# Attention and slot mixture on one core: one PSUM bank per product, ScalarE rounds the pair sums, and four engines get new orders

## The chip, the core and the metric

One core of a Trainium2 chip runs the whole program. Its engines work side by side, each through its own list of instructions in order: TensorE (PE, with weight loads as PEld), VectorE (DVE), ScalarE (ACT), GpSimd (POOL) and SyncE (SP, which here only issues transfers). They meet at semaphores. PSUM has eight banks of 2 KB per partition, in which PE leaves its products and which ACT and DVE read. The metric is the device time of one execution in microseconds; lower is better.

## The reference

```python
x = L0_attn_x                                        # 32 x 256 x 128
# attention, linear and causal: 16 heads of 8
q, k, v = exp(ln(x) @ Wq.T + bq), exp(ln(x) @ Wk.T + bk), ln(x) @ Wv.T + bv
kv = cumsum(k[..., :, None] * v[..., None, :], over the sequence); k1 = cumsum(k)
att = (q @ kv) / (q . k1)
x = x + ln(att @ Wo.T + bo)
# slot mixture: 8 experts x 64 slots = 512 slots
xn, se = rms_norm(ln(x)), rms_norm(slot_embeds)
logits = xn @ se.T                                   # 256 x 512
slots = softmax(logits, over tokens).T @ xn
processed = gelu(slots @ w1) @ w2
x = x + ln(softmax(logits, over slots) @ processed)
```

All is float32. There are 32 batches of 256 tokens.

## The kernel before

A batch is one unit of work. Its 256 tokens lie on 128 partitions, two neighbours (an even and an odd token) on each. A product that has to be exact is split: an operand is rounded to a high part (`_hi`) and the rest is its low part (`_lo`), and `three` multiplies hi by hi, hi by lo and lo by hi. Each engine's program is a list of calls such as `hidden(n, f)`, where `n` is the batch. `first_steps` and `last_steps` write out the ends of the program, and `step(s)` the steady part. One step works on up to seven batches at different stages.

One batch passes through the engines so. DVE takes the statistics of x (`x_statistics`), POOL makes 1/sqrt of the variance (`x_rstd_of`, an operation on two numbers per partition), DVE normalises (`x_normalise`), PE transposes (`x_transpose`), ACT copies the rounded part (`xT_high`) and DVE the rest (`xT_low`). `project` makes q, k and v, `v_evict` and `qk_evict` (with exp) move them to `E`. SP then copies the odd tokens' keys and values one partition further down, into `prev` (`shift_odd`, two transfers of 112 and 15 KB). POOL makes the outer products of keys and values (`outer_even`, `outer_odd`), adds them (`pair_sum`, `pair_keys`) into `kv` (128 x 1152), copies it rounded to `kv_hi` (`sums_high`) and subtracts (`sums_low`). `cumulate` multiplies both with a triangle, in three parts k = 0, 1, 2. DVE multiplies each part by q (`multiply`) and sums over the head (`attention_sums`), and `attention` divides. `att_transpose`, `attT_copy` and `attention_out` follow, then the squares on ACT (`y_squares`), the power on POOL (`y_rstd_of`), `first_residual` on DVE, and the same for the second normalisation: `x1_squares`, `x1_rstd_of`, `x1_normalise`, `xn_transpose`, `xnT_high`, `xnT_low`.

The mixture goes on with `logits`, the two maxima on DVE (`slot_maxima`, `part_maxima`), `dispatch_exp` on ACT, `dispatch_scale` on DVE, `dispatch_transpose`, `dispatch_copy` on ACT, `gather_slots`, `slT_high` (ACT), `slT_low` (DVE), `hidden` in four parts with a `gelu` each, `process`, `proc_copy`, `mixture` and, after one more set of squares and power, `second_residual`. ACT loads a table before the first gelu of a step and again before the exps (`gelu_table`, `exp_table`).

PSUM is held as four pairs of banks: WB, LA, LB and HB. WB serves `x_transpose`, `att_transpose`, `project`, `part_transpose`, `attention_out`, `cumulate`, `xn_transpose` and the sums of the attention, one after another. So `project(n, 1)` waits until ACT has copied the transposed attention of batch n - 2 out of the bank:

```python
elif c == 1:
    after(pe, attT_ready, n - 2)
...
three(WB[:, c, 0:QKV], xT_hi[:, cols], xT_lo[:, cols], wqkv_hi[:, :], wqkv_lo[:, :])
```

`hidden` uses the two banks of HB in turn, so parts 2 and 3 wait for the gelus of parts 0 and 1. `wait_ge(s, v)` is a wait, `then_inc` an engine's signal on completion, and `after(eng, s, n)` waits until batch n has signalled `s`. In an order, `waits s_attT` means `attT_ready`, and so on.

Of the kernel before, what the change touches and what calls it, by code (L numbers as in the profile page):

```python
# [5 lines left out]
def attention_and_slot_mixture(  # L6
# [45 lines left out]
    with ctx:  # L52
# [6 lines left out]
        def sem(name):  # L59
# [89 lines left out]
        LBv = LB[:, :, :].rearrange("p g (j t) -> p (g j) t", t=SEQ)  # L149
        OB = LA[:, :, 0:YW]  # L150
        PR = HB[:, 0, :].rearrange("p (j d) -> p j d", d=DIM)
        ND = WB[:, 1, 0:NC * (HD + 1) * NH].rearrange("p (c f h) -> p c f h", c=NC, h=NH)
        YB = WB[:, 1, 0:NC * YW].rearrange("p (c d) -> p c d", d=YW)
# [3 lines left out]
        s_wT, s_woT, s_wop, s_wu, s_sesum, s_senorm, s_kappa = (  # L157
            sem("s_" + n) for n in ("wT", "woT", "wop", "wu", "sesum", "senorm", "kappa"))
        s_gxs, s_sefloor, s_sehi, s_wqkvhi, s_wqkv, s_w1hi, s_wo_t = (
            sem("s_" + n) for n in ("gxs", "sefloor", "sehi", "wqkvhi", "wqkv", "w1hi", "wo_t"))  # L160
# [15 lines left out]
        xT_lo_ready, qk_exp, kv_even, kv_odd, kv_den, kv_built = (  # L176
            sem("s_" + n) for n in ("xTlo", "qkexp", "kve", "kvo", "kvd", "kv"))
        kv_hi_ready, kv_lo_ready, qk_own_ready, own_den, own_ready, own_added = (
            sem("s_" + n) for n in ("kvhi", "kvlo", "qkown", "ownden", "own", "ownadd"))
        summed, den_ready, att_ready, att_T, attT_ready, wo_done = (  # L180
            sem("s_" + n) for n in ("summed", "deninv", "att", "attTp", "attT", "wo"))
        y_var, y_rstd, x1_ready, x1_var, x1_floor, x1_rstd = (
            sem("s_" + n) for n in ("yve", "yrs", "x1", "x1ve", "x1fl", "x1rs"))
        xn_ready, xnT_done, xnT_hi_ready, xnT_lo_ready, lb_done, part_ready = (
            sem("s_" + n) for n in ("xn", "xnT", "xnThi", "xnTlo", "lb", "part"))
        partT_done, tok_ready, lb_shifted, disp_exp, disp_inverted, disp_scaled = (
            sem("s_" + n) for n in ("partT", "tok", "lbs", "dexp", "dinv", "dscale"))
        slT_done, slT_hi_ready, slT_lo_ready, proc_ready, mix_done, o_var = (
            sem("s_" + n) for n in ("slT", "slThi", "slTlo", "procs", "mix", "ove"))
        o_rstd, res_ready, x_stat = (  # L190
            sem("s_" + n) for n in ("ors", "res", "xstat"))
# [28 lines left out]
        def _(sp):  # L220
# [43 lines left out]
        def _(pool):  # L264
# [17 lines left out]
            def x_rstd_of(n):  # L282
                pool.wait_ge(x_stats, n + 1)
                if n == 2:
                    after(pool, xh_ready, n - 1)
# [9 lines left out]
            def wo_order():  # L295
                pool.wait_ge(s_woload, 16)
                pool.tensor_copy(wo_p[:, :].rearrange("p (d h) -> p d h", d=HD),
                                 w_in[:, 3, :].rearrange("p (h d) -> p d h", d=HD)).then_inc(s_wop, 1)

            def slot_norms():  # L300
                pool.wait_ge(s_sesum, 1)
# [5 lines left out]
            @each_batch  # L307
            def sums_high(n):
                after(pool, cum_done[2], n - 1)
                if n == 1:  # L310
                    pool.wait_ge(kv_den, n + 1)
                pool.wait_ge(kv_built, n + 1)
                pool.tensor_copy(kv_hi[:, :], kv[:, :]).then_inc(kv_hi_ready, 1)
# [8 lines left out]
            def own_value(n):  # L322
                pool.wait_ge(own_den, n + 1)
# [30 lines left out]
            def outer_even(n):  # L354
                if n == 0:
                    pool.wait_ge(qk_exp, n + 1)
                if n == 1:
                    after(pool, kv_lo_ready, n - 1)
# [4 lines left out]
            def outer_odd(n):  # L363
                if n == 1:
                    after(pool, kv_built, n - 1)
                loaded(pool, prev_loaded, n, 2)
# [4 lines left out]
            def pair_keys(n):  # L371
                u = n % 2
# [12 lines left out]
            def first_steps():  # L385
                wo_order()
                slot_norms()
# [4 lines left out]
                outer_odd(1)  # L392
                outer_even(1)
                pair_sum(1)
                x_negative(1)
                pair_keys(1)
                own_value(0)
                sums_high(1)
                sums_low(1)
                own_product(1)  # L400
                x_rstd_of(3)
                y_rstd_of(0)
                outer_odd(2)
                x1_rstd_of(0)
                x_negative(2)
                own_value(1)
                outer_even(2)
                pair_keys(2)
                pair_sum(2)
                own_product(2)  # L410
                sums_high(2)
                sums_low(2)
                y_rstd_of(1)
                x_rstd_of(4)
                outer_odd(3)
# [1160 lines left out]
```

## Time and profile before

| | |
|---|---|
| median of 3 runs | 620.16 us (617.2 to 620.59) |
| profiled execution | 618.45 us, span of the core 616.7 us |
| PE busy | 586.3 us, 95% of the span |
| POOL busy | 501.2 us, 81% |
| DVE busy | 488.9 us, 79% |
| ACT busy | 448.1 us, 73% |
| TensorE clock granted | full in all of the steady part |

Busy is the union of an engine's instructions, so two matmuls that overlap in the pipeline count once. The steady part repeats with each batch, so one step of it, from one `gather_slots` to the next, is the unit in which the trace is read.

### The profile page before, as it was taken

To read this page: it belongs to the slowest core of one execution; us is meant where nothing else is said; L and a number is where in the kernel's file an instruction comes from. 1 tells how busy PE (TensorE), PEld (TensorE's weight loads), DVE (VectorE), ACT (ScalarE), POOL (GpSimd) and SP (SyncE) were. 2 spreads that over 40 slices of the span, in tenths; PEclk is the share of its full clock that TensorE was granted. 3 is DMA by queue.
4 is the path that set the end of the run, shared out by engine and by line. 5 is a ranking of instruction groups with operands and counts; after the bars stand their busy time and mean duration, and the time that the engine had idled before them with its cause. 6 is when DMAs were issued, how large, how long until landed. Compare 5 with 4: busy or idle time off the path is not lost.

```text
span 616.7 us, 10792 instructions
## 1 busy us (share of the span) xinstructions
PE 586.3 (95%) x3884; PEld 498.7 (81%) x3884; DVE 488.9 (79%) x922; ACT 448.1 (73%) x1213; POOL 501.2 (81%) x493
## 2 busy tenths in 40 slices
PE   7988999999999999999999999999999999999986
PEld 7976888888888888888888888888888888887775
DVE  6778788888888888888888888888888888877630
ACT  4046787877777878777778787777787877777763
POOL 5589898898888988988889899888898898985100
PEclk9999999999999999999999999999999999999999
DMA  4000000000000000000000000010000000000000
GB/s 111 10 19 19 18 17 10 27 18 25 27 27 27 25 10 27 19 27 26 27 28 27 10 25 18 27 27 25 27 27 11 26 17 27 19 27 9 10 10 17
DMA packets 16825, 14.29 MB, mean 23 GB/s; under 512 B 2850, under 2 KB 16644, under 8 KB 16772
## 3 DMA queue, kind: packets, MB, share of 16 engines
q1 hardware_dynamic: 14708, 12.76, 6.9%
q10 hardware_dynamic: 2064, 0.86, 0.5%
q8 instruction: 30, 0.49, 0.4%
q14 instruction: 23, 0.19, 0.1%
HBM read 5.25 MB, written 4.19 MB: 15 GB/s over the span
## 4 chain that ended last, share of the span: by engine, by line
PE 45%; ACT 34%; POOL 8%; DVE 4%; issue 3%; DMA 0%; DVEq 0%; POOLq 0%; SPq 0%
PE HB L984 10%; ACT disp_t L660 9%; PE LA L1004 9%; POOL y_rs L333 7%; PE HB L849 5%; ACT disp L550 5%; PE HB L851 5%; PE HB L850 5%; ACT L558 4%; ACT x_sq L595 4%; DVE x L1351 3%; PE WB L849 3%; ACT y_sq L587 3%; ACT E L610 2%; ACT hid L570 2%
## 5 line engine op out<-in xcount | busy, mean ns | idle before, releaser
L993 PE MATMUL HB<-w_c,hid 128*128 128x128 f32 x1024 | 124.9, 275 | 2.3 <-ACT hid L570 2.3
L993 PEld LDWEIGHTS HB<-w_c,hid 128*128 128x128 f32 x1024 | 121.1, 192 | 3.6 <-ACT hid L570 3.6
L1311 DVE TENSOR_TENSOR prod<-WB,E 128x768 f32<-128x768 f32 x96 | 88.3, 949 | 3.6 <-PE WB L937 3.6
L570 ACT ACTIVATE hid<-HB 128x512 f32<-128x512 f32 x128 | 76.2, 598 | 14.0 <-PE HB L851 5.8
L1329 DVE TENSOR_REDUCE WB<-prod 128x288 f32<-128x2304 f32 x32 | 82.0, 2561 | 1.1
L318 POOL TENSOR_TENSOR kv_lo<-kv,kv_hi 128x1152 fp32r<-128x1152 f32 x31 | 81.8, 2638 | 0.2
L984 PE MATMUL HB<-disp,xn 128*128 128x512 f32 x128 | 63.3, 617 | 12.7 <-ACT disp L550 12.6
L379 POOL TENSOR_TENSOR kv<-kv,kv_prev 128x1024 f32<-128x1024 f32 x31 | 74.6, 2405 | 0.1
L204 POOL TENSOR_TENSOR kv_prev<-prev 128x1024 f32<-128x1024 f32 x31 | 66.5, 2145 | 9.4 <-DMA prev<-E 9.3
L204 POOL TENSOR_TENSOR kv<-E 128x1024 f32<-128x1024 f32 x32 | 68.5, 2140 | 1.4 <-ACT E L610 1.3
L333 POOL TENSOR_TENSOR y_rs<-y_ve,minus_half 128x2 f32<-128x2 f32 x32 | 45.0, 1407 | 29.4 <-ACT y_sq L587 29.4
L1004 PE MATMUL LA<-proc,comb 128*128 128x129 f32 x512 | 62.5, 274 | 0.8 <-ACT proc L550 0.8
L1004 PEld LDWEIGHTS LA<-proc,comb 128*128 128x128 f32 x512 | 59.9, 191 | 1.9 <-issue 1.9
L660 ACT ACTIVATE disp_t<-LB,neg_max 128x256 f32<-128x256 f32 x128 | 59.0, 486 | 0.0
L849 PE MATMUL HB<-slT_hi,w_hi 128*128 128x512 f32 x128 | 56.2, 439 | 0.5 <-ACT hid L570 0.3
L984 PEld LDWEIGHTS HB<-disp,xn 128*128 128x128 f32 x128 | 21.8, 189 | 37.5 <-ACT disp L550 22.0
L850 PE MATMUL HB<-slT_lo,w_hi 128*128 128x512 f32 x128 | 50.6, 395 | 0.0
L851 PE MATMUL HB<-slT_hi,w_lo 128*128 128x512 f32 x128 | 50.5, 394 | 0.0
L550 ACT ACTIVATE proc<-HB 128x512 f32<-128x512 f32 x32 | 19.1, 598 | 38.3 <-PE HB L993 38.3
L345 POOL TENSOR_TENSOR o_rs<-o_ve,minus_half 128x2 f32<-128x2 f32 x32 | 22.3, 697 | 30.3 <-ACT o_sq L604 30.3
L550 ACT ACTIVATE slT_hi<-HB 128x512 fp32r<-128x512 f32 x32 | 19.1, 597 | 30.9 <-PE HB L984 30.9
L554 ACT ACT_TABLE_LOAD x32 | 41.1, 1283 | 0.6
(138 smaller groups left out, 1595.6 us busy)
## 6 DMA issues: line engine op xcount, KB each, us to landing
X<-in_L_attn_x_dram SPq DMA_DIRECT2D x32, 128.0 KB, 2.1
out_dram<-res SPq DMA_DIRECT2D x32, 128.0 KB, 2.0
prev<-E SPq DMA_DIRECT2D x32, 112.0 KB, 2.2
w_in<-in_L_ffn_w_dram ACTq DMA_DIRECT2D x2, 256.0 KB, 4.5
prev<-E SPq DMA_DIRECT2D x32, 15.0 KB, 2.0
se_in<-n_L_ffn_slot_embeds_dram ACTq DMA_DIRECT2D x1, 256.0 KB, 3.6
w_in<-in_L_attn_Wq_dram SPq DMA_DIRECT2D x1, 64.0 KB, 2.4
w_in<-in_L_attn_Wk_dram SPq DMA_DIRECT2D x1, 64.0 KB, 2.1
```

What stands on the lines that cost most here:

```text
L204: return eng.tensor_tensor(dst.rearrange("p (d h e) -> p d h e", d=HD, h=NH), k.rearrange("p (o h e) -> p o h e", o=1, h=NH).broadcast_to( ...
L318: pool.tensor_tensor(kv_lo[:, :], kv[:, :], kv_hi[:, :].bitcast(F32), ALU.subtract)\
L333: pool.tensor_tensor(y_rs[:, :], y_ve[:, :], minus_half[:, 0:NC], ALU.pow).then_inc(y_rstd, 1)
L570: act.activation(hid[:, f, :], HB[:, f % 2, :], ACT.Gelu).then_inc(gelu_ready[f], 1)
L660: last = act.activation(disp_t[:, j, :], LBv[:, j, :], ACT.Exp, bias=neg_max[:, j:j + 1], accum_out=disp_sum[:, j:j + 1])
L849: pe.matmul(dst, a_hi, b_hi, start=start, stop=False, skip_group_check=True)
L850: pe.matmul(dst, a_hi, b_lo, start=False, stop=False, skip_group_check=True)
L984: last = pe.matmul(HB[:, 0, :], xn[n % 2][:, c, :], disp[:, c, :], start=(c == 0), stop=(c == NC - 1))
L993: last = pe.matmul(PR[:, j, :], hid[:, f, j * P:(j + 1) * P], w2_c[:, f, :], start=(f == 0), stop=(f == FJ - 1))
L1004: last = pe.matmul(OB[:, c, :], comb[n % 2][:, j, c * P:(c + 1) * P], proc[:, j, 0:YW], start=(j == 0), stop=(j == SJ - 1))
L1311: dve.tensor_tensor(prod[u][:, :, d0 * DIM:d1 * DIM].rearrange("p c (d f) -> p c d f", d=g), WB[:, k % 2, 0:g * DIM].rearrange("p (o d f) ...
L1329: dve.tensor_reduce(ND.rearrange("p c f h -> p c (f h)"), prod[n % 2][:, :, :].rearrange("p c (f e) -> p c f e", e=HD), AX.X, ALU.add).the ...
```

## The change

Four things are changed. The pairs of banks go: one tensor of eight banks is cut by hand, so that most products have a bank that no other product beside them uses, and many waits for a free bank go or change.

```diff
-        WB = pb("WB", [P, 2, 512])
-        LA = pb("LA", [P, 2, 512])
-        LB = pb("LB", [P, 2, 512])
-        HB = pb("HB", [P, 2, 512])
+        banks = pb("banks", [P, 8, 512])
+        WB = banks[:, 0:2, :]
+        LB = banks[:, 2:4, :]
+        XT = banks[:, 1, 0:SEQ]
+        XN = banks[:, 3, 0:SEQ]
+        PT = banks[:, 7, 0:SEQ]
+        CU = [banks[:, 6, 0:DU * DIM], banks[:, 5, 0:DU * DIM], banks[:, 5, 0:DU * DIM]]
+        ND = banks[:, 7, 0:NC * (HD + 1) * NH].rearrange("p (c f h) -> p c f h", c=NC, h=NH)
+        AT = banks[:, 7, 0:SEQ]
+        YO = banks[:, 4, 0:NC * YW]
+        DT = [banks[:, 0, :], banks[:, 7, :]]
+        SL = banks[:, 0, :]
+        HP = [banks[:, 6, :], banks[:, 0, :], banks[:, 6, :], banks[:, 4, :]]
+        PR = banks[:, 6, :].rearrange("p (j d) -> p j d", d=DIM)
+        OB = banks[:, 5, 0:NC * YW].rearrange("p (c d) -> p c d", d=YW)
```

`sums_high` moves from POOL to ACT, and SP's `shift_odd` waits for the copy of v instead of the exp of q and k, since ACT now makes v last:

```diff
-                pool.tensor_copy(kv_hi[:, :], kv[:, :]).then_inc(kv_hi_ready, 1)
+                act.wait_ge(kv_built, n + 1)
+                copy(kv_hi[:, :], kv[:, :]).then_inc(kv_hi_ready, 1)
...
-                sp.wait_ge(qk_exp, n + 1)
+                sp.wait_ge(v_copied, n + 1)
```

The waits of PE that the new banks bring or drop:

```diff
 project
-                    after(pe, attT_ready, n - 2)
+                    after(pe, gelu_ready[1], n - 4)
 part_transpose
-                after(pe, qk_exp, n + 3)
+                after(pe, attT_ready, n + 1)
 dispatch_transpose
+                    after(pe, v_copied, n + 3)
 xn_transpose
+                after(pe, comb_ready[1], n - 1)
 cumulate
+                    after(pe, proc_ready, n - 3)
+                    pe.wait_ge(prod_ready[2], n + 1)
+                    after(pe, res_ready, n - 4)
 mixture
+                after(pe, prod_ready[1], n + 3)
```

And the orders of PE, ACT, DVE and POOL are new, with fewer idle products (`spin`) of PE in the first steps (one run of 40 before the first `cumulate`) and `bo_centre` later on DVE. On ACT, the stretch from the gelus of one batch to the copies of `disp` reads before:

```order
L570 ACTIVATE hid<-HB 128x512 [waits s_hid3]
L558 ACT_TABLE_LOAD
L550 ACTIVATE attT<-WB 128x256 [waits s_attTp]
L550 ACTIVATE E<-WB 128x2x128 [waits s_proj1]
L610 ACTIVATE E<-WB 128x2x256
L660 ACTIVATE disp_t,disp_sum<-LB,neg_max 128x256 [waits s_part]
L660 ACTIVATE disp_t,disp_sum<-LB,neg_max 128x256 x3
L587 ACTIVATE y_sq,y_ve<-WB 128x129 [waits s_wo]
L587 ACTIVATE y_sq,y_ve<-WB 128x129
L550 ACTIVATE proc<-HB 128x4x128 [waits s_proc1]
L595 ACTIVATE x_sq,x_v<-x_1,neg_m 128x128 [waits s_x1]
L595 ACTIVATE x_sq,x_v<-x_1,neg_m 128x128
```

and with the change, where `banks` is the one PSUM tensor:

```order
L430 ACT_TABLE_LOAD
L422 ACTIVATE kv_hi<-kv 128x1152 [waits s_kv]
L491 ACTIVATE E<-banks 128x2x256 [waits s_proj1]
L422 ACTIVATE attT<-banks 128x256 [waits s_attTp]
L545 ACTIVATE disp_t,disp_sum<-banks,neg_max 128x256 [waits s_part]
L545 ACTIVATE disp_t,disp_sum<-banks,neg_max 128x256 x3
L422 ACTIVATE E<-banks 128x2x128
L464 ACTIVATE y_sq,y_ve<-banks 128x129 [waits s_wo]
L464 ACTIVATE y_sq,y_ve<-banks 128x129
L422 ACTIVATE proc<-banks 128x4x128 [waits s_proc1]
L422 ACTIVATE disp<-banks 128x512 [waits s_dispT0]
L422 ACTIVATE disp<-banks 128x512 [waits s_dispT1]
```

`kv_hi` comes in behind the table load, the copy of v moves behind the four exps of the dispatch, and both copies of `disp` stand ahead of the squares of x1.

On POOL, the middle of a step reads before, from the two instructions of `x1_rstd_of` on:

```order
L338 TENSOR_SCALAR x_vf<-x_v 128x2 [waits s_x1ve]
L340 TENSOR_TENSOR x_rs<-x_vf,minus_half 128x2 [waits s_x1fl]
L292 TENSOR_SCALAR neg_m<-x_mv 128x2
L325 TENSOR_TENSOR own<-E,own 128x128 [waits s_ownden]
L204 TENSOR_TENSOR kv<-E 128x1024
L373 TENSOR_TENSOR kv<-E,prev 128x128
L379 TENSOR_TENSOR kv<-kv,kv_prev 128x1024 [waits s_kve]
L350 TENSOR_TENSOR qk_own<-E 128x128
L313 CAST kv_hi<-kv 128x1152 [waits s_kv,s_cum2]
```

and with the change, one row earlier on:

```order
L212 TENSOR_TENSOR kv_prev<-prev 128x1024 [waits prev_loaded1]
L339 TENSOR_SCALAR x_vf<-x_v 128x2 [waits s_x1ve]
L341 TENSOR_TENSOR x_rs<-x_vf,minus_half 128x2 [waits s_x1fl]
L374 TENSOR_TENSOR kv<-E,prev 128x128
L300 TENSOR_SCALAR neg_m<-x_mv 128x2
L212 TENSOR_TENSOR kv<-E 128x1024
L326 TENSOR_TENSOR own<-E,own 128x128
L380 TENSOR_TENSOR kv<-kv,kv_prev 128x1024 [waits s_kve]
```

Behind the power that DVE's `x1_normalise` waits for, POOL no longer waits for DVE's `own_sum` but goes straight on with `pair_keys` and `outer_even`.

On PE, the stretch from the gather to the projection of one step reads with the change:

```order
L929 MATMUL banks<-disp,xn 128x512 [waits s_disp1]
L929 MATMUL banks<-disp,xn 128x512
L955 MATMUL banks<-proc,comb 128x129 [waits s_prod1]
L955 MATMUL banks<-proc,comb 128x129 x7
L889 MATMUL banks<-ident,xn 128x128 [waits s_comb1,s_xn]
L889 MATMUL banks<-ident,xn 128x128
L802 MATMUL banks<-slT_hi,w_hi 128x512 [waits s_slTlo]
```

where before the transpose of xn stood ahead of the mixture:

```order
L984 MATMUL HB<-disp,xn 128x512 [waits s_disp1]
L984 MATMUL HB<-disp,xn 128x512
L943 MATMUL WB<-ident,xn 128x128 [waits s_xn]
L943 MATMUL WB<-ident,xn 128x128
L1004 MATMUL LA<-proc,comb 128x129 x8
L849 MATMUL HB<-slT_hi,w_hi 128x512 [waits s_slTlo]
```

`xn_transpose` has moved 1.8 us of PE's work later, behind the mixture, and has a second wait, for the last exp that reads its bank.

## Rows read from the trace of the kernel before

**Rows 1.** The page: busy time, share of the span and instructions of each engine.

```profile
PE 586.3 (95%) x3884; PEld 498.7 (81%) x3884; DVE 488.9 (79%) x922; ACT 448.1 (73%) x1213; POOL 501.2 (81%) x493
```

**Rows 2.** Busy time of each engine in one step of the steady part.

```profile
303.05:320.66 17.61, 17.17 (x113) 14.56 (x113) 14.83 (x30) 13.75 (x38) 15.81 (x16) 1.00 0.08 23
```

**Rows 3.** Timeline of PE in that step: start, us, instruction, idle before and releaser.

```profile
302.33 0.34 PE L937 MATMUL WB<-kv_lo,tri 128*128 128x384 f32 x1
303.05 1.99 PE L984 MATMUL HB<-disp,xn 128*128 128x512 f32 x4 [0.39 <-ACT disp L550]
...
306.80 0.48 PE L849 MATMUL HB<-slT_hi,w_hi 128*128 128x512 f32 x1
...
309.93 0.28 PE L849 MATMUL LB<-xnT_hi,se_hi 128*128 128x256 f32 x1
...
311.25 0.28 PE L851 MATMUL LB<-xnT_hi,se_lo 128*128 128x256 f32 x1
...
312.09 0.34 PE L851 MATMUL WB<-wqkv_hi,xT_lo 128*128 128x384 f32 x1
312.48 0.44 PE L849 MATMUL WB<-wqkv_hi,xT_hi 128*128 128x384 f32 x1
```

**Rows 4.** The chain that ended last, in the same step: start, us, what.

```profile
310.13 0.60 ACT hid L570
310.74 1.28 ACT L558
312.04 0.39 ACT attT L550
...
312.92 0.17 PE WB L850
...
314.18 1.82 ACT disp_t L660 x8
...
319.65 0.97 ACT disp L550 x2
```

**Rows 5.** Timeline of PE: the first gather, the gather of batch 28.

```profile
55.86 1.88 PE L984 MATMUL HB<-disp,xn 128*128 128x512 f32 x4
```

```profile
549.71 1.98 PE L984 MATMUL HB<-disp,xn 128*128 128x512 f32 x4 [0.40 <-ACT disp L550]
```

**Rows 6.** Groups of instructions: busy us, mean ns of one, idle before.

```profile
L1329 DVE TENSOR_REDUCE WB<-prod 128x288 f32<-128x2304 f32 x32 | 82.0, 2561 | 1.1
...
L1370 DVE TENSOR_REDUCE part_max<-LB 128x256 f32<-128x1024 f32 x32 | 38.9, 1215 | 0.0
...
L313 POOL CAST kv_hi<-kv 128x1152 fp32r<-128x1152 f32 x31 | 35.7, 1151 | 0.1
...
L340 POOL TENSOR_TENSOR x_rs<-x_vf,minus_half 128x2 f32<-128x2 f32 x32 | 23.9, 746 | 2.7
...
L1238 DVE TENSOR_TENSOR slT_lo<-HB,slT_hi 128x512 fp32r<-128x512 f32 x32 | 22.1, 690 | 12.6 <-ACT slT_hi L550 12.5
...
L550 ACT ACTIVATE slT_hi<-HB 128x512 fp32r<-128x512 f32 x32 | 19.1, 597 | 30.9 <-PE HB L984 30.9
```

**Rows 7.** The chain early on: SP's first issue, the second's transfer.

```profile
34.41 0.52 SPq L235
...
34.97 3.01 DMA prev<-E
```

**Rows 8.** All 64 issues into `prev`: us to landing.

```profile
DMA to landing us min/median/max: 2.0/2.1/3.7
```

**Rows 9.** Timelines of POOL and of DVE where `outer_odd` meets `x_normalise`.

```profile
38.05 2.13 POOL L204 TENSOR_TENSOR kv_prev<-prev 128x1024 f32<-128x1024 f32 x1 [1.28 <-DMA prev<-E]
```

```profile
39.38 1.16 DVE L1217 TENSOR_SCALAR xh<-X,x_mv,x_rs 128x128 f32<-128x128 f32 x2
41.41 0.60 DVE L1359 TENSOR_SCALAR xn<-x,x_mv,x_rs 128x128 f32<-128x128 f32 x2 [0.88 <-POOL x_rs L340]
```

**Rows 10.** Timeline of PE: the second projection.

```profile
17.56 0.44 PE L849 MATMUL WB<-wqkv_hi,xT_hi 128*128 128x384 f32 x1 [0.35 <-DVE xT_lo L1275]
```

More of the change, by code:

```diff
@@ L182, in attention_and_slot_mixture @@
[L182 to L189, printed above, removed]
@@ L392, in first_steps @@
                 outer_odd(1)
+                slot_norms()
+                pair_keys(1)
                 outer_even(1)
+                own_value(0)
                 pair_sum(1)
[L395 to L398, printed above, removed]
+                own_product(1)
                 sums_low(1)
[L400 to L415, printed above, removed]
-                x1_rstd_of(1)
-                x_negative(4)
-                x_negative(3)
-                own_value(2)
-                outer_even(3)
-                pair_keys(3)
@@ L456, in first_steps @@
-                own_value(5)
-                outer_even(6)
-                pair_keys(6)
-                pair_sum(6)
-                sums_high(6)
-                x_rstd_of(8)
-                o_rstd_of(2)
-                sums_low(6)
-                y_rstd_of(5)
-                outer_odd(7)
-                x1_rstd_of(5)
-                own_product(6)
-                x_negative(7)
-                outer_even(7)
-                own_value(6)
-                pair_keys(7)
-                pair_sum(7)
@@ L771, in last_steps @@
-            def last_steps():
+                gelu(1, 2)
+                gelu(1, 3)
+                exp_table(6)
+                sums_high(4)
+                qk_evict(5)
+                attT_copy(3)
+                dispatch_exp(2)
+                v_evict(5)
+                y_squares(3)
+                proc_copy(1)
+                dispatch_copy(2, 0)
+                dispatch_copy(2, 1)
+                x1_squares(3)
+                combine_exp(2, 0)
+                xT_high(6)
+                slT_high(2)
@@ new lines, in first_steps @@
+                combine_exp(2, 1)
+                gelu_table(2)
+                xnT_high(3)
+                o_squares(1)
+                gelu(2, 0)
+                gelu(2, 3)
+                gelu(2, 1)
+                gelu(2, 2)
+                exp_table(7)
+                sums_high(5)
+                v_evict(6)
+                attT_copy(4)
+                qk_evict(6)
+                dispatch_exp(3)
+                y_squares(4)
+                proc_copy(2)
+                dispatch_copy(3, 0)
@@ L821, in _ @@
             first_steps()
-            for s in range(5, 33):
+            for s in range(8, 33):
                 step(s)
@@ L1185, in _ @@
             first_steps()
-            for s in range(5, 31):
+            for s in range(6, 32):
                 step(s)
@@ L1445, in first_steps @@
                 part_maxima(0)
-                token_maxima(0)
-                own_sum(2)
-                dispatch_scale(0)
-                first_residual(1)
-                multiply(2, 0)
-                multiply(2, 1)
-                multiply(2, 2)
-                x_normalise(4)
-                x1_normalise(1)
-                slT_low(0)
-                x_statistics(5)
-                xnT_low(1)
-                attention_sums(2)
-                attention(2)
-                xT_low(4)
@@ L1539, in step @@
+                multiply(s - 2, 2)
                 first_residual(s - 3)
```

730 lines of the change are left out of this document (316 added, 414 removed).

## Prediction

> **What bounds the kernel now.** I read the page first, then one step of the steady part, then the chain that ended last, and at the end what the new order leans on. PE is busy for 95% of the span and no other engine above 81% [rows 1]. In one step of 17.61 us PE is busy 17.17 us, POOL 15.81, DVE 14.83 and ACT 13.75 [rows 2]. So PE is nearly full, and the most that any order can bring is what PE still waits.
>
> PE's timeline shows two waits per step [rows 3]. A product 384 wide lets its successor start 0.17 us after it [rows 4], so after the last one of `cumulate`, at 302.33, the gather could start at 302.50. It starts at 303.05: 0.55 us, and the row names the copy of `disp` on ACT. The second half of `project` could start at 312.09 + 0.18 and starts at 312.48: 0.21 us, behind the copy of the transposed attention. Together 0.76 us, so PE's own work is 17.61 - 0.76 = 16.85 us per step.
>
> The chain says who is late [rows 4]: gelu 0.60, table load 1.28, copy of attT, projection, copies of E, four exps of the dispatch 1.82, squares, the power on POOL, residual, squares of x1, two copies of `disp` 0.97, then the gather and `hidden` on PE, and round again. That is one loop through ACT and PE of exactly one step, closed by ACT's order and by `project` waiting for `attT_copy`.
>
> From the first gather at 55.86 to that of batch 28 at 549.71 [rows 5] there are 28 steps of 17.64 us on average. Ahead lie 55.9 us, behind (616.7 - 549.7) 67.0 us.
>
> **The loop is cut.** With the change `project` no longer waits for the attention's copy, and both copies of `disp` stand ahead of the squares of x1, which need the power from POOL. The loop above exists no more. If nothing else takes its place a step costs 16.85 us: 28 x 0.76 = 21.3 us less. That is the ceiling for the steady part.
>
> **The rounded copy.** POOL loses `sums_high`, 1.15 us per batch [rows 6]. No ACT row of this size exists. ACT took 0.39 us for 256 columns [rows 4] and 0.597 for 512 [rows 6], 0.83 ns a column more, which gives 1.13 us for 1152; the bounds are 1.0 and 1.4. ACT's busy time then is 13.75 + 1.13 = 14.9 us of 16.85, so ACT isn't full. But the copy stands between the table load and `qk_evict`, and POOL's `sums_low` now waits for it. Counting from the start of `logits`: the last gelu ends about 0.8 us in, the table load at 2.1, the copy at 3.2, then `qk_evict` and `attT_copy` end at 3.9. The first exp of the dispatch needs both maxima. `logits` ends at 1.60 (309.93 to 311.25 and 0.28 [rows 3]), the maxima take twice 1.2 [rows 6], 2.36 with overlap, so they end at 4.0. The copy is hidden by 0.1 us of slack; a cost of 1.4 us would put 0.2 us on the loop below, 5 us in all.
>
> **The new loop.** I follow what is late next, again from the start of `logits`. Exps begin at 4.0 and end at 5.85 (1.82). Only then does ACT copy v, to 6.25. SP, which waits for it, issues two transfers: 0.52 us for the first, then the second, whose landing takes 2.0 us at best [rows 7, 8]. With the hops the two are there at about 8.95. POOL's `outer_odd` takes 2.13 [rows 9], then `x1_rstd_of`, which stands behind it, 0.75 [rows 6] and 0.45 for the clamp and gaps: 12.3. `x1_normalise` 0.5, `slT_low` 0.69 [rows 6]: 13.55, and `hidden` may start. `hidden` to `logits` is 309.93 - 306.80 = 3.13 less the transpose of x (0.2) that has left it: 2.92. The loop closes at 16.5 us. The branch through `attention_sums` (2.56 [rows 6]) and `xnT_low` closes at 16.5 too. So with a fast landing PE's 16.85 rules, by 0.35 us. Before, POOL began `outer_odd` well after the landing and this transfer cost nothing; now nothing covers it.
>
> It isn't always fast. Half the landings take 2.1 us or less, the longest 3.7 [rows 8]; an early one took 3.01 [rows 7]. Of 29 steps from batch 3 on, the small transfer took 3.0 to 3.7 us in 9 and 2.0 in 20. A landing 1.3 us later (3.3 for 2.0) gives 17.8, 0.95 above PE's work. I take 1.1 us for such a step, with the hand-over below: 9 x 1.1 = 10 us back. Bounds: 0, if landings keep clear, and 28 us, if each of 28 is late by 1.0.
>
> **DVE against POOL.** At 39.38 two normalisations of DVE take 1.16 us, while `outer_odd` runs on POOL to 40.18; at 41.41 two alike, with POOL nearly idle, take 0.60 [rows 9]. The first waited until POOL's long instruction was over. In the new order `x1_normalise` starts when the power ends, and so does `pair_keys` (0.45 us), with `outer_even` (2.1) behind. If DVE's second half waits for `pair_keys` only, the loop is 16.95 instead of 16.5: 0.1 us over PE. I put 0.1 us on each of 28 steps for this and the other thin places (the gather has 0.15 us behind the second copy of `disp`, part 2 of `hidden` 0.1 behind its gelu): 3 us, bounds 0 and 8.
>
> On this the Trainium skill (SBUF — State Buffer, "Who interferes with whom") says that VectorE in a two-port mode and GpSimd hold a shared pair of ports as a lock for a whole instruction, and that the order of issue decides who is blocked. The trace agrees in the pair at 39.38. By this rule alone the worst case is the rival below, in which the second half loses to `outer_even`.
>
> **The other waits.** The remaining new waits have slack. `cumulate` part 2 waits for `sums_low`, done at 3.3 + 2.6 = 5.9, and comes at 7.3. `dispatch_transpose` comes at 8.2 and the scale is done at 7.4. `mixture` comes at 11.9 and `multiply` part 1 is done at 11.55. `xn_transpose` comes at 13.6 and the last exp from its bank is done at 13.2. `project` waits for a gelu done at 0.1. A late landing only widens these. POOL works 15.81 - 1.15 = 14.7 us per step and stays below 16.85.
>
> **The ends.** Before, the second projection waits to 17.56 for `xT_low` [rows 10], which stands behind `bo_centre` on DVE; now it comes at about 14. Part of it is used up: the squares of the slots go ahead of an exp on ACT, and PE spins 40 times before the first `cumulate`. I carry 3 us to the first gather, between 0 and 5. At the end the gathers of batches 29 to 31 are bound by the exps and the scale of the dispatch, as before; only the first interval falls towards PE's work. 1.5 us, between 0 and 3.
>
> **Sum.** 21.3 - 10 - 3 = 8.3 in the steady part, 3 and 1.5 at the ends: 12.8 us. The profiled execution took 618.45, so 605.7 by it. It lies 1.7 us below the median of the runs, which spread over 3.4 us; I take 605.
>
> **The rivals.** First, PE full: the landings keep clear and the hand-over costs nothing. Then 21.3 + 4.5 = 25.8, about 593. For it speaks that 20 of 29 landings were fast and that every engine but PE has 2 us to spare; against it, a loop with 0.35 us of slack. Second, the transfer or the hand-over binds in every step: steps of 17.4 to 17.6, 0 to 6 us of gain there, 608 to 616. Third, no change: a wait that I hold covered takes 0.9 us in every step, and the new loop is as long as the old; 617 to 622. Fourth, slower: the second half of `x1_normalise` loses to `outer_even` in each step and waits 2.1 us longer. The loop is 16.5 + 0.3 + 2.15 = 18.95, 1.3 above the step of before: 28 x 1.3 - 4.5 = 32 us more, about 651. It decides once the loop of 16.5 grows by over 1.3 us (21.3 + 4.5 is 0.92 per step, on top of the slack of 0.35). Against it: when `pair_keys` ends, the half is already waiting, and the next on POOL is the tiny `x_negative`.
>
> **How the numbers follow.** Forecast (598 to 608) 0.42, PE full (590 to 598) 0.25, bound in every step (608 to 617) 0.17, no change 0.06, slower 0.10. Within 0.5% of 620.16 means 617.1 to 623.3, about what a measurement of this kernel can tell from no change. Faster is then 0.84, the same 0.06, slower 0.10. The range 591 to 615 holds the first three.
>
> **What would show it.** PE's gather no longer waits 0.4 us for ACT, and `project` never for attT. Steps come in two lengths, 16.9 and 17.5 to 18.2; in the long ones POOL waits for `prev` ahead of `outer_odd`, and PE ahead of `hidden`, of `xn_transpose` or of `logits`. ACT's copy of `kv` takes 1.13 us. The two halves of `x1_normalise` together take 0.6 to 1.1 us. The prediction is wrong in its core if steps are longer than 17.6, if POOL's wait for `prev` goes together with no wait of PE, or if a wait for a bank shows on PE that I hold covered.

## Result and profile after

The changed kernel takes 594.8 us, the median of 4 runs (594.5 to 595.7), against 619.6 us for the kernel before on the same chip: a ratio of 0.961 with an interval of [0.958, 0.964]. The prediction was 605 in a range of 591 to 615. The profiled execution took 594.6 with a span of 592.9.

The page of the changed kernel, first part, to be held against [rows 1]:

```profile
PE 557.5 (94%) x3772; PEld 486.1 (82%) x3772; DVE 484.2 (82%) x922; ACT 473.4 (80%) x1244; POOL 473.1 (80%) x462
```

One step of the steady part, from gather to gather, as in [rows 2]:

```profile
307.53:324.31 16.78, 16.49 (x115) 14.46 (x114) 14.65 (x29) 14.56 (x39) 14.92 (x15) 1.00 0.08 25
```

The step is 16.78 us for 17.61. The first gather is at 56.16 (before 55.86 [rows 5]), that of batch 28 at 525.39 (before 549.71), and 67.5 us follow it (before 67.0). So all of the gain, 24.6 us, is in the 28 steady steps, and nothing came at the two ends. From the fourth on nearly all steps are 16.78 long; one is 17.31, the gather of 189.53 to that of 206.84.

PE's timeline at the end of a step, where [rows 3] showed the gather waiting 0.39 us for ACT:

```profile
323.64 0.44 PE L881 MATMUL banks<-kv_hi,tri 128*128 128x384 f32 x1 [0.29 <-DVE prod L1253]
...
324.31 1.88 PE L929 MATMUL banks<-disp,xn 128*128 128x512 f32 x4
```

The gather (L929) follows its predecessor without a gap, and `project` too. What waits is the last part of `cumulate` (L881), 0.29 us, for DVE's `multiply` (L1253): one small wait per step, and another one than any of the prediction's. It is a wait for a bank, and the change itself brought it: `CU[1]` and `CU[2]` are both `banks[:, 5, ...]`, so part 1 of `cumulate` may start only when DVE has multiplied part 2 out of that bank (`pe.wait_ge(prod_ready[2], n + 1)`). The chain that ended last, in this step (start, us, what), says where it comes from:

```profile
314.29 0.60 ACT hid L447
...
314.91 1.28 ACT L430
...
316.20 1.17 ACT kv_hi L422
...
317.44 2.64 POOL kv_lo L318
...
320.44 1.66 POOL x_rs L296
...
322.12 0.60 DVE xh L1157 x2
322.72 0.88 DVE prod L1253
```

After the last gelu comes the table load, then ACT's rounded copy (`kv_hi`, 1.17 us), for which POOL's `sums_low` (`kv_lo`) waits. Behind it on POOL stand the two instructions of `x_rstd_of`, behind these DVE's `x_normalise` (`xh`) and the first `multiply` (`prod`), and then PE: `cumulate`, gather, mixture, `hidden`, and the next gelu. The loop closes at 16.78 us and goes through the very copy that was moved.

One number in it is odd. The power (L296), an operation on 2 numbers per partition, takes 1.66 us. Here it stands beside DVE's work in the next step:

```profile
337.23 1.63 POOL L296 TENSOR_TENSOR x_rs<-x_ve,minus_half 128x2 f32<-128x2 f32 x1
```

```profile
337.08 1.23 DVE L1331 TENSOR_TENSOR disp_t<-disp_t,disp_inv 128x1024 f32<-128x1024 f32 x1
338.90 0.60 DVE L1157 TENSOR_SCALAR xh<-X,x_mv,x_rs 128x128 f32<-128x128 f32 x2 [0.59 <-POOL x_rs L296]
```

POOL's power begins 0.15 us after DVE's `dispatch_scale` (L1331) and ends 0.55 us after it. The groups of POOL show that it is so on average, and how little is left of the transfer that the prediction feared (busy us, mean ns of one, idle before):

```profile
L212 POOL TENSOR_TENSOR kv_prev<-prev 128x1024 f32<-128x1024 f32 x31 | 66.8, 2153 | 10.5 <-DMA prev<-E 10.5
L296 POOL TENSOR_TENSOR x_rs<-x_ve,minus_half 128x2 f32<-128x2 f32 x32 | 47.9, 1495 | 2.7
L334 POOL TENSOR_TENSOR y_rs<-y_ve,minus_half 128x2 f32<-128x2 f32 x32 | 24.0, 751 | 13.2 <-ACT y_sq L464 13.2
```

The power of the same form in `y_rstd_of` takes 0.75, the one beside `dispatch_scale` 1.50. POOL waits 10.5 us for the transfer in the whole run, and of 29 landings one was late (2.8 us), where before 9 were.

### The profile page after: what moved, and what is told of

It is laid out like the page before. It is cut to its first block, busy times and chain, and to the rows that moved or that the text cites. A ratio compares the mean times of both kernels' runs of the same rounds, so it can differ in the third digit from the quotient of the medians.

```text
span 592.9 us, 10573 instructions
## 1 busy us (share of the span) xinstructions
PE 557.5 (94%) x3772; PEld 486.1 (82%) x3772; DVE 484.2 (82%) x922; ACT 473.4 (80%) x1244; POOL 473.1 (80%) x462
## 4 chain that ended last, share of the span: by engine, by line
PE 42%; POOL 23%; ACT 19%; DVE 10%; issue 3%; DMA 1%; SPq 0%; POOLq 0%; DVEq 0%; ACTq 0%
POOL kv_lo L318 11%; PE banks L929 9%; PE banks L955 8%; POOL x_rs L296 7%; ACT kv_hi L422 6%; ACT L430 6%; PE banks L802 5%; PE banks L804 5%; PE banks L803 5%; DVE prod L1253 4%; ACT hid L447 3%; DVE xh L1157 3%; PE banks L782 3%; PE banks L881 2%; ACT disp_t L545 2%
## 5 line engine op out<-in xcount | busy, mean ns | idle before, releaser
L942 PE MATMUL banks<-w_c,hid 128*128 128x128 f32 x1024 | 124.6, 276 | 2.4 <-ACT hid L447 2.4
L942 PEld LDWEIGHTS banks<-w_c,hid 128*128 128x128 f32 x1024 | 119.2, 192 | 3.5 <-ACT hid L447 2.2
L1253 DVE TENSOR_TENSOR prod<-banks,E 128x768 f32<-128x768 f32 x96 | 88.3, 948 | 1.9 <-PE banks L882 1.9
L1268 DVE TENSOR_REDUCE banks<-prod 128x288 f32<-128x2304 f32 x32 | 81.5, 2545 | 0.0
L212 POOL TENSOR_TENSOR kv_prev<-prev 128x1024 f32<-128x1024 f32 x31 | 66.8, 2153 | 10.5 <-DMA prev<-E 10.5
L955 PEld LDWEIGHTS banks<-proc,comb 128*128 128x128 f32 x512 | 61.1, 191 | 17.0 <-DVE prod L1253 14.9
L447 ACT ACTIVATE hid<-banks 128x512 f32<-128x512 f32 x128 | 70.5, 612 | 4.8 <-PE banks L804 2.0
L955 PE MATMUL banks<-proc,comb 128*128 128x129 f32 x512 | 62.5, 275 | 0.8 <-ACT proc L422 0.8
L929 PE MATMUL banks<-disp,xn 128*128 128x512 f32 x128 | 60.7, 597 | 1.1 <-ACT disp L422 1.0
L545 ACT ACTIVATE disp_t<-banks,neg_max 128x256 f32<-128x256 f32 x128 | 58.9, 474 | 0.0
L802 PE MATMUL banks<-slT_hi,w_hi 128*128 128x512 f32 x128 | 54.7, 427 | 0.2 <-DVE slT_lo L1178 0.2
L881 PE MATMUL banks<-kv_hi,tri 128*128 128x384 f32 x96 | 41.4, 432 | 10.7 <-DVE prod L1253 9.3
L296 POOL TENSOR_TENSOR x_rs<-x_ve,minus_half 128x2 f32<-128x2 f32 x32 | 47.9, 1495 | 2.7
```

The costliest lines, as they stand in the source:

```text
L212: return eng.tensor_tensor(dst.rearrange("p (d h e) -> p d h e", d=HD, h=NH), k.rearrange("p (o h e) -> p o h e", o=1, h=NH).broadcast_to( ...
L296: pool.tensor_tensor(x_rs[:, :], x_ve[:, :], minus_half[:, 0:NC], ALU.pow).then_inc(x_rstd, 1)
L447: act.activation(hid[:, f, :], HP[f], ACT.Gelu).then_inc(gelu_ready[f], 1)
L802: pe.matmul(dst, a_hi, b_hi, start=start, stop=False, skip_group_check=True)
L929: last = pe.matmul(SL, xn[n % 2][:, c, :], disp[:, c, :], start=(c == 0), stop=(c == NC - 1))
L942: last = pe.matmul(PR[:, j, :], hid[:, f, j * P:(j + 1) * P], w2_c[:, f, :], start=(f == 0), stop=(f == FJ - 1))
```

## The theories

**Theory A.** The step is 16.78 because of the loop above: ACT's copy, `sums_low`, then the stretched power. PE's own work lies a little below. **Rival B**: PE's own work is the 16.78, or another loop is, and the wait of 0.29 is only what shows first. The first run moves `x_rstd_of` out of the loop, the second makes only the half of that move which shouldn't matter, and the third takes the moved copy back to POOL.

### x_rstd_of ahead of sums_low

```diff
 # DVE, in step(s)
-                x_statistics(s)
                 attention(s - 2)
+                x_statistics(s + 1)
                 slot_maxima(s - 3)
 # POOL, in step(s)
-                x_rstd_of(s)
                 own_product(s - 1)
+                x_rstd_of(s + 1)
                 sums_low(s - 1)
```

> The changed kernel, with DVE's x_statistics of the next batch moved ahead of slot_maxima (where DVE waited 0.96 us for the logits) and POOL's x_rstd_of of that batch ahead of sums_low (where POOL waited 1.05 us for the rounded copy). Theory A, the step of 16.78 us is a loop gelu, table load, rounded copy on ACT, sums_low, power x_rs (1.65 us, held up by DVE's dispatch_scale), x_normalise, multiply part 2, last cumulate, gather, hidden: the loop loses the two x_rs instructions, x_rs shrinks to 0.7 us, PE's wait of 0.3 us for multiply part 2 goes and a step takes 16.4 to 16.5 us, 584 to 588 us in all. Theory B, PE is full at 16.78 and its 0.3 us of idle is only how the pipeline is drawn: no change, 594 to 596.

590.3 us, ratio 0.954 [0.950, 0.957], span 588.6, 4.3 us less than the changed kernel's. The direction is A's, the size short of the 584 to 588 expected. The step is 16.55 us and PE is busy for all of it:

```profile
305.50:322.05 16.55, 16.55 (x115) 14.60 (x113) 14.79 (x29) 14.56 (x39) 14.46 (x15) 1.00 0.08 25
```

So 16.55 is PE's own work in a step, and the loop had cost 0.23 us per step, 6.4 us in 28. Of this 1.8 us went back here in two steps, one of 17.91 behind a late landing (3.4 us) and the last, of 16.99, whose landings took 2.1. The power ahead of `x_normalise` is at 706 ns again; `y_rstd_of` stands beside `dispatch_scale` now and takes 1,148 instead of 751:

```profile
L334 POOL TENSOR_TENSOR y_rs<-y_ve,minus_half 128x2 f32<-128x2 f32 x32 | 36.7, 1148 | 30.8 <-ACT y_sq L465 30.8
```

### Only the statistics early

The DVE half of the same edit, with `x_rstd_of` left behind `sums_low`.

> Only the DVE half of the edit: x_statistics of the next batch ahead of slot_maxima, POOL's order as in the changed kernel. Theory A: POOL still makes x_rs behind sums_low, so the loop is untouched, 594 to 596. If DVE as a whole were the limit (theory C), filling its idle 0.96 us would bring up to 0.67 us per step, 576 to 580.

595.4 us, ratio 0.961 [0.959, 0.963]: no change. The gain of the run before was the power's place on POOL.

### The rounded copy back on POOL

```diff
 # POOL
+            def sums_high(n):
+                after(pool, cum_done[1], n - 1)
+                pool.wait_ge(kv_den, n + 1)
+                pool.wait_ge(kv_built, n + 1)
+                pool.tensor_copy(kv_hi[:, :], kv[:, :]).then_inc(kv_hi_ready, 1)
 # ACT: the copy is gone, its wait stands ahead of qk_evict and v_evict
-            def sums_high(n):
-                act.wait_ge(kv_built, n + 1)
-                copy(kv_hi[:, :], kv[:, :]).then_inc(kv_hi_ready, 1)
```

> The changed kernel with the rounded copy back on POOL, directly ahead of sums_low; ACT keeps the wait for the pair sums that ordered it against POOL, but not the copy. Theory A: POOL now waits 1.05 us for ACT at this place, the copy takes 1.15 us there, so sums_low starts 0.1 to 0.2 us later and a step grows by as much: 596 to 600. Theory D, taking the copy off POOL is what made the kernel faster: POOL's 1.15 us come back in every step, 622 to 628.

599.3 us, ratio 0.966 [0.963, 0.969]: 3.9 us slower than the run before, which was measured side by side with it and times like the changed kernel. So 20.9 of the 24.7 us gained are there without the move and come from the banks and the orders together. No run has the new banks with the old orders, so how they share it is not shown. With the copy on POOL the chain goes through that copy, `sums_low` and the power's first instruction, which is now the one that is stretched (1.26 for 0.20):

```profile
306.85 1.26 POOL x_ve L294
```

### Three moves in the kernel before

With the old banks: the copies of `disp` ahead of the squares of x1, the table load ahead of `xnT_high`, the mixture ahead of `xn_transpose`.

```diff
-                x1_squares(s - 2)
                 dispatch_copy(s - 3, 0)
                 dispatch_copy(s - 3, 1)
+                x1_squares(s - 2)
...
-                xnT_high(s - 2)
                 gelu_table(s - 3)
+                xnT_high(s - 2)
...
-                xn_transpose(s - 2)
                 mixture(s - 4)
+                xn_transpose(s - 2)
```

> The kernel before, with its shared banks, and three moves in the steady part: both copies of disp ahead of the squares of x1, the gelu table ahead of xnT_high (both on ACT), mixture ahead of xn_transpose on PE. If the old loop through ACT's order was the limit, its cut brings most of the gain without new banks: the gather no longer waits 0.55 us, the wait of project for attT (0.21) stays, POOL comes close to its limit: steps of 17.1 to 17.3, 606 to 611. If the banks are what counts: 617 to 620.

612.3 us, ratio 0.988 [0.985, 0.991], a little less of a gain than the 606 to 611 expected. The step is 17.34 us. In the stretch below its chain is nearly the loop that the prediction had drawn for the changed kernel: v copy, SP, the landing, `outer_odd`, power, `x1_normalise`.

```profile
312.69 0.38 ACT E L550
...
314.18 3.54 DMA prev<-E
...
317.79 2.15 POOL kv_prev L204
...
320.41 0.73 POOL x_rs L340
```

The landing takes 3.54 us here, and the chain goes through it. But it isn't what makes the step 17.34. In the step from 406.51 to 423.83 both landings take 2.1 us, POOL doesn't wait for them, and it is as long (17.32). There the chain runs from the copies of `disp` through the squares of x1, the power and `x1_normalise` to the sums of the attention (L1329), and through `att_transpose` (L884) back to PE:

```profile
405.40 0.60 ACT disp L550
406.00 0.77 ACT x_sq L595 x4
...
411.31 2.57 DVE WB L1329
...
415.19 0.44 PE WB L884 x2
```

Seven of this kernel's steps have a landing of 3.3 us or more. One of them is followed by a step of 17.69, the others by 17.36 to 17.42, so they cost little here. The three moves alone bring 7.8 us, held against 24.8 for the whole change.

### The squares of x1 ahead of both copies of disp

The changed kernel with the one order undone that, by the prediction, cuts the old loop.

```diff
+                x1_squares(s - 3)
                 dispatch_copy(s - 4, 0)
                 dispatch_copy(s - 4, 1)
-                x1_squares(s - 3)
```

> The changed kernel with one thing of ACT's old order back in the steady part: the squares of x1 ahead of both copies of disp. Theory A: the loop then runs on from multiply part 2 through first_residual, the squares (0.9 us) and the copies (1.0 us) to the gather, which comes 1.8 us later: steps of 18.5 to 18.7, 640 to 648 us. If PE's queue absorbs it (theory B, PE full and nothing else near): under 600.

666.4 us, ratio 1.076 [1.073, 1.079]: worse than the kernel before, and 18 us beyond the expected range. The old loop is back, as theory A says: in every step the gather now waits 1.55 us for the copies of `disp`. But from the fifth to the 27th the steps come in two lengths, nine of 19.2 us and fourteen of 20.2 to 20.3. Below stand the gather of one of each and two stretches behind the wait of the second (length, busy us of PE, PEld, DVE, ACT and POOL with counts, granted clock, DMA share, GB/s):

```profile
322.28 1.98 PE L929 MATMUL banks<-disp,xn 128*128 128x512 f32 x4 [1.55 <-ACT disp L422]
341.49 3.62 PE L929 MATMUL banks<-disp,xn 128*128 128x512 f32 x4 [1.55 <-ACT disp L422]
```

```profile
341.45:343.30 1.85, 1.81 (x3) 0.78 (x4) 1.07 (x2) 0.75 (x2) 1.70 (x4) 0.56 0.04 13
343.30:345.20 1.90, 1.90 (x5) 0.87 (x4) 1.88 (x2) 0.05 (x1) 1.90 (x3) 0.53 0.00 0
```

In the long steps the granted clock reads 0.56 and 0.53 behind the wait, close to 1.2 GHz for 2.4, and the gather takes 3.62 us instead of 1.98. Fourteen times 1.04 us is 14.5 us, most of the 18 by which the expectation fell short; it had left the clock out. Why PE kept its full clock behind the same wait in nine steps, the runs do not show.

In those nine steps another thing shows, a mechanism that had been one of the prediction's rivals:

```profile
320.39 0.88 ACT x_sq L472 x4
321.27 0.96 ACT disp L422 x2
...
323.45 2.57 DVE xn L1299 x2
```

Two halves of `x1_normalise` (L1299) take 2.57 us, where they take 0.74 in the changed kernel. On POOL `outer_even` runs just then; DVE's pair starts at 323.37, 0.05 us behind it:

```profile
323.32 2.13 POOL L212 TENSOR_TENSOR kv<-E 128x1024 f32<-128x1024 f32 x1
```

From the gather to `hidden` PE takes 4.39 us here (322.28 to 326.67) for 3.64 in the changed kernel. So the stretch costs 0.75 us at most, and 19.2 less 0.75 is 18.45, about what the expectation had for the reordering alone. In the long steps the low clock covers it. This is the mechanism of the prediction's slower rival (18.95 us a step, 651 us), but it isn't what makes this kernel slow: the loop through the squares and the clock are. The changed kernel doesn't show it, though a move of two small ACT instructions is enough to call it up, and the expectation had left it out.

### ACT makes the rounded copy twice

```diff
+                copy(kv_twice[:, :], kv[:, :])
                 copy(kv_hi[:, :], kv[:, :]).then_inc(kv_hi_ready, 1)
```

Nobody reads `kv_twice`. The edit is made once in the changed kernel and once in the faster order of the first experiment.

> The changed kernel; ACT makes the rounded copy of the pair sums twice, first into a tile that nobody reads. Theory A, the copy lies on the binding loop: 1.07 us more in each of 28 steps, 30 us, 622 to 627. Theory B, PE full at 16.78: 594 to 596.

625.8 us, ratio 1.012 [1.009, 1.014], 31.0 us more than the changed kernel. 27.1 of it are in the 28 steps, which have grown to 17.74; 2.7 lie ahead of the first gather and 1.2 behind the last of the 28. That is 0.96 us a step. The second copy adds 1.06 to the loop, and the stretched power gives 0.11 back (1.55 for 1.66). So the copy lies on the path that binds, without slack, and theory A stands.

> The faster order of e1_power_early (x_rstd_of ahead of sums_low) in which ScalarE makes the rounded copy twice, the second into a tile that nobody reads. Theory A (in that order the rounded copy has left the path that binds; TensorE's own 16.55 us a step binds, and the copy has some slack of its own): the copy of 1.07 us more moves attT and the exponentials behind it, the first of which has about 0.4 us to spare, so a step grows by 0.4 to 0.8 us and the time is 600 to 613 us, less than the 31 us that the same copy cost in e6_copy_twice. Rival B (the copy binds there too, by another way): 619 to 622 us, 31 us above the 590 of e1_power_early. Rival C (it has a full microsecond to spare): below 594 us.

619.0 us, ratio 1.002 [1.000, 1.004]: 28.7 us more than without the second copy and in rival B's range; a steady step is 0.95 us longer. Theory A was wrong here: it took the copy to have left the critical region with `x_rstd_of`. It has left one loop and stands in another, a little shorter one, which is the one that the prediction had worked out:

```profile
326.74 0.60 ACT hid L450
...
328.65 1.17 ACT kv_twice L424
329.82 1.05 ACT kv_hi L424
...
333.75 0.56 SPq L246
334.35 2.04 DMA prev<-E
336.46 2.15 POOL kv_prev L213
...
339.00 0.72 POOL x_rs L342
339.75 0.75 DVE xn L1302 x2
```

From the end of one gelu (327.34) to the end of the next (344.84) it closes at 17.5 us. Without the 1.05 of the second copy that is 16.45 (an estimate from this kernel's rows); the prediction had 16.5. So with the faster order PE's 16.55 and this loop lie 0.1 us apart. There the first copy is hidden by about as much as the prediction had said for the changed kernel, but one more of 1.05 us isn't free in either order.

### The scale of the dispatch behind the power

To test the stretched power by itself: DVE's `dispatch_scale` no longer runs beside it.

```diff
-                dispatch_scale(s - 4)
                 x_normalise(s)
                 multiply(s - 2, 2)
+                dispatch_scale(s - 4)
                 first_residual(s - 3)
```

> The changed kernel with dispatch_scale moved behind x_normalise and the first part of multiply on VectorE. Theory A (the power under x_rs takes 1.66 us only because VectorE's dispatch_scale, with its two operands in SBUF, runs at the same time): the power reads 0.70 us here, x_normalise no longer waits 0.59 us for it, and what stands under dispatch_scale now (y_rs or kv_prev) is stretched in its place. As for the time: TensorE's dispatch transposes now stand behind power 0.70, x_normalise 0.6, multiply 0.95 and dispatch_scale 1.23, and 2.3 us of its own work follow them to the gather, so each step is 1.5 to 1.9 us longer, 637 to 648 us in all. Rival B (the power is slow for a reason of its own in this order, for instance because it reads what VectorE has just written): it still reads 1.5 us or more with dispatch_scale elsewhere, and the time is 660 us or more.

683.6 us, ratio 1.105 [1.102, 1.107]. The duration is as theory A says, the time is 36 us beyond its upper end. POOL's groups:

```profile
L212 POOL TENSOR_TENSOR kv_prev<-prev 128x1024 f32<-128x1024 f32 x31 | 85.7, 2764 | 38.0 <-DMA prev<-E 38.0
...
L296 POOL TENSOR_TENSOR x_rs<-x_ve,minus_half 128x2 f32<-128x2 f32 x32 | 22.5, 704 | 2.7
```

The power is back at 704 ns, and `outer_odd` (`kv_prev`), which now stands beside `dispatch_scale`, has gone from 2,153 to 2,764. The stretch belongs to whatever POOL starts while `dispatch_scale` runs. The Trainium skill (SBUF — State Buffer, "Who interferes with whom") states such a rule: a VectorE instruction with two inputs in SBUF contends with a GpSimd instruction that reads SBUF, since its second input comes through a port pair that the two share, and that pair is an exclusive lock that goes by the order of issue. The trace agrees in five kernels here: the one before (`y_rs`), the changed one (`x_rs` of x), the first experiment (`y_rs`), the copy back on POOL (`x_ve`) and this one.

What the expectation missed comes with PE's wait. The 28 steps take 553.2 us for 469.2, 19.76 each, 3.0 more than in the changed kernel where 1.5 to 1.9 were expected. In the step looked at PE waits 2.02 us for `dispatch_scale`. One step, then four stretches from its wait on:

```profile
317.90:337.57 19.67, 17.65 (x114) 15.71 (x114) 14.49 (x29) 14.57 (x39) 14.79 (x15) 0.93 0.07 21
```

```profile
332.00:334.60 2.60, 0.63 (x5) 0.43 (x4) 2.57 (x6) 0.46 (x1) 1.34 (x2) 1.00 0.18 50
334.60:337.50 2.90, 2.85 (x14) 2.78 (x15) 1.18 (x3) 1.99 (x7) 1.90 (x1) 0.61 0.28 90
337.50:339.80 2.30, 2.30 (x6) 1.08 (x5) 1.91 (x5) 0.72 (x2) 2.02 (x5) 0.75 0.00 0
339.80:345.00 5.20, 5.20 (x34) 4.53 (x33) 4.28 (x6) 4.87 (x12) 5.20 (x5) 1.00 0.01 3
```

Behind the stretch in which PE worked 0.63 us the granted clock reads 0.61 and 0.75, a mixture of 1.2 and 2.4 GHz, and then 1.00 again. The eight transposes take 1.42 us for 1.04. From the transposes to the gather it is 2.92 us, for 2.05 in the changed kernel without its wait; from the gather to the mixture 2.25 for 1.72. How much of the low clock falls into a step varies, so its price is read from PE's busy time in a whole one: 17.65 us for 16.49, 1.2 us a step or about 33 us in 28. The rest of the 3.0, about 1.8, is the wait and lies inside the expectation. Of the 36 us above the expected range 31 are in the 28 steps, and 4.3 lie ahead of the first gather (60.46 for 56.16).

### The start

The first gather comes no earlier than before, where the prediction put 3 us. PE's first steps in the changed kernel, rows that wait:

```profile
31.21 0.67 PE L832 MATMUL banks<-ident,att 128*128 128x128 f32 x2 [1.97 <-DVE att L1281]
34.65 0.58 PE L863 MATMUL banks<-b_rows,ones_r 128*128 128x258 f32 x1 [2.77 <-DVE b_rows L1206]
```

PE waits for DVE again and again, and from 30 to 50 us the granted clock is 0.50 to 0.67. The next run only fills these waits with idle products (`spin`), with three waits for the banks that they write; the last adds a new order of the first steps to the first experiment (`bo_centre` and `w2_centre` earlier, `x_normalise` of batch 3 later).

```diff
                 slot_transpose()
+                spin(9)
                 att_transpose(0)
+                spin(12)
                 attention_out(0)
...
```

> The changed kernel with idle products put back on PE in the first 55 us, where PE waits and its granted clock falls to 0.5 (30 to 48 us of the span). If the low clock costs time at the start: the logits, the third projection and the copies behind them come earlier, 1 to 4 us, 591 to 594. If DVE and POOL set the pace there anyway: 594 to 596.

594.7 us, ratio 0.961 [0.958, 0.963], with the clock at 1.00 from 20 to 55 us. The first gather is at 54.92, 1.2 us earlier, and yet nothing is gained: four of the steady steps have grown, to 17.67, 17.53, 17.16 and 17.57, and the 28 together take 471.9 us for 469.2. In each of the four POOL waits 0.95 to 1.45 us for the transfer, where it waits 0.30 in the others. POOL's timeline in the first of them:

```profile
154.63 2.13 POOL L212 TENSOR_TENSOR kv_prev<-prev 128x1024 f32<-128x1024 f32 x1 [1.43 <-DMA prev<-E]
```

These are the long steps of the prediction, and the landings ahead of them took 2.7 to 3.2 us. The changed kernel has one before batch 28, the one with only the statistics moved none, and their number varies between kernels whose steady part is the same.

> The kernel of e1 (power early) with a new start: bo_centre before the first outer product, w2_centre on ACT behind the second exp, x_normalise(3) behind two multiplies, 32 idle products for 40, and idle products where PE waits. The first gather should come at 52 to 53 instead of 56.2: 586 to 588 us. If the start is not on the path: 590.

589.7 us, ratio 0.952 [0.949, 0.955]; measured side by side it lies 5.0 us below the run before, just what the first experiment gained without the new start. The first gather is at 54.93, 1.8 us earlier than in the first experiment, and three steps behind a late landing (17.2 to 17.7) take most of it back, where the first experiment had one. So the start holds 1 to 2 us, below what these runs can tell. These two orders are the fastest versions, 5 us below the changed kernel.

## Why the prediction was right, and what in it was not

The measured 594.8 lies in the range of 591 to 615, but 10 us below the forecast of 605 and outside the band that the prediction held likeliest (598 to 608). The direction and the cut of the old loop came out as reasoned. The size is the sum of errors that partly cancel.

**The ceiling, 21.3 us.** Mis-sized: the steady part gave 24.6, more than the "ceiling", and PE's own work is 16.55, not 16.85. The step counted two waits. But work without waits also got shorter, by the groups before (first fence) and after (second):

```profile
L963 PE MATMUL LA<-ident,disp_t 128*128 128x128 f32 x256 | 39.6, 279 | 0.7 <-DVE disp_t L1389 0.6
...
L849 PE MATMUL WB<-wqkv_hi,xT_hi 128*128 128x384 f32 x64 | 28.0, 438 | 2.0 <-ACT attT L550 0.4 <-DVE xT_lo L1275 0.4
```

```profile
L910 PE MATMUL banks<-ident,disp_t 128*128 128x128 f32 x256 | 33.4, 274 | 2.3 <-DVE disp_t L1331 2.3
...
L802 PE MATMUL banks<-wqkv_hi,xT_hi 128*128 128x384 f32 x64 | 22.4, 350 | 0.3 <-DVE xT_lo L1217 0.2
```

The transposes of `disp_t` stood in two runs of 4 with a piece of `cumulate` between; in one run of 8 they lose 0.19 us per batch (6.2 in 32). The first products of a projection lose 0.17 (5.6 in 32). Before, one took 0.45 us behind a transpose and the other 0.44 behind its wait; in the changed kernel each follows a product that is not a transpose, without a wait, and takes 0.34. That is 0.36 per step, which the two-wait count couldn't see, and covers the difference of 0.30.

**The loop is cut.** Right. The gather and `project` no longer wait, and with the squares put back ahead of the copies the gather waits 1.55 us again and the step grows to 19.2 or 20.2.

**The rounded copy, "hidden by 0.1 us of slack".** The duration was right: 1.13 forecast, 1.165 measured. That it was hidden is the step that failed. The text followed ACT behind the copy, and found `cumulate` part 2 covered, but didn't follow POOL behind `sums_low`: `x_rstd_of`, which stands there, is what `x_normalise` waits for, with the first `multiply` behind it, and so the last part of `cumulate`. The link between those two is the bank that parts 1 and 2 share, and the paragraph on the other waits doesn't have it. By the prediction's own last sign, a wait for a bank on PE, this is where it was wrong. No run gives part 1 another bank, so whether that alone would open the loop is not shown. The loop cost 0.23 us a step over PE's own work, and a second copy 31 us in all. The text also weighed POOL against DVE for `x1_normalise` alone and didn't ask what stands beside `dispatch_scale`; that adds 0.95 us to this loop, which by these rows would close at 15.8 without it (an estimate) and stay below PE.

**The new loop of 16.5 us.** Right as a mechanism and in size, as the second kernel with two copies shows (16.45), but not what binds the changed kernel: POOL's wait for the transfer went with no wait of PE, which the prediction had named as a sign against itself.

**Late landings, 10 us.** Mis-sized by the count: one of 29 was late, for 9 before, and cost 0.5 us. The length of a step behind a late landing, 17.5 to 18.2 in the prediction, was 17.2 to 17.9 in four kernels that show one to four of them. What makes a landing late no run here settles.

**The hand-over, 3 us.** Mis-sized for `x1_normalise` (0.74 for two halves, 0.14 above the undisturbed pair [rows 9], and off the path), but real elsewhere: the loop's 0.23 per step are 6.4 us.

**The ends, 4.5 us.** Wrong by all of it: -0.3 and -0.5. The second projection does come at 13.76 instead of 17.56 [rows 10], but the waits for DVE come after it, and the prediction had looked at none of them. At the end the first interval does fall, from 17.04 to 16.49, but the next grows from 15.82 to 17.31, where PE waits 1.05 us for a gelu and 1.35 for the scale of the dispatch. The last was held to be as before.

In sum, between the profiled executions: (17.64 - 16.55) x 28 = 30.5 us from PE, less 5.9 in the steps that the new loop and the one landing lengthen, less 0.8 at the ends, 23.8 us; forecast were 12.8. Of the difference of 11, 9.2 is the larger ceiling, 7.1 the smaller losses in the steps (5.9 for 13), and 5.3 was lost at the ends. The measured time lies in the rival "PE full". Its condition on the landings held in 28 of 29, but PE isn't quite full, and it came to 593 with a ceiling that was too low by 9: its number was met partly by luck.

## What to carry to other kernels

When work is moved from one engine to another, follow the queue behind whoever waits for it, not only the queue it is put into: here the copy's consumer was covered, and an instruction on two numbers behind the consumer closed the loop. For every small POOL instruction on a path, look what DVE runs at that moment; an instruction of DVE with two operands in SBUF doubled its time here. To move the small one ahead of `sums_low` cost nothing, while to move DVE's instruction instead made PE wait 2.0 us a step. When a wait of PE grows, read the granted clock behind it before the size is explained: in two kernels here it made up 14.5 and about 33 us. And a bound "own work = step minus waits" leaves out what a wait or an interleaved order adds to the durations next to it; here that was 9 us beside a gain of 25.

## What the runs showed of the hardware

- A POOL power on 2 numbers per partition takes 0.70 us, and 1.50 on average (up to 1.66) when DVE's product of two SBUF operands of 1,024 columns runs beside it. In the same way DVE's two halves of `x1_normalise` take 2.57 for 0.74 us when POOL's `outer_even` of 2.13 us starts first.
- In the kernel with a wait of PE of 2.0 us in each step the granted clock reads 0.61 and 0.75 in the 5.2 us behind the wait, and PE is busy 1.2 us longer in a step. With a wait of 1.55 us it reads 0.56 and 0.53 in the long steps, fourteen of 23, each 1.0 us longer than the nine others. The kernels whose longest wait in a step is 0.3 to 0.6 us read 1.00 throughout the steady part.
- A granted clock of 0.50 to 0.67 over 20 us at the start cost 1.2 us at the first gather, because DVE sets the pace there.
- The same small transfer inside SBUF was late in 9 of 29 steps in one order, in 1 of 29 in another, and in four with the same steady part and other first steps. This remains open.
